# Rounded down products in six of sixteen groups of a sort stage

## The reference

```python
x = x + 0.5 * _L0_ffn_ref(_layernorm(x), expert_sel, keys, values)    # first time
x = x + _L0_attn_ref(...)                                              # linear attention
x = x + 0.5 * _L0_ffn_ref(_layernorm(x), expert_sel, keys, values)    # second time: the first sort stage
x = x + 0.5 * _L1_ffn_ref(...)                                         # mixture of 8 experts, top 2
x = x + _L1_attn_ref(...)
x = x + 0.5 * _L1_ffn_ref(...)
```

```python
gates = sigmoid(xt @ expert_sel.T)                   # all but the top 4 set to 0: gate_full
scores = relu(einsum('nd,edf->nef', xt, keys)) * gate_full[:, :, None]
out = einsum('nef,efv->nv', scores, values)
```

## Time and profile before

| | us |
|---|---|
| median of 3 runs | 1647.75 (1647.23 to 1655.29) |
| profiled execution, its own time | 1646.87 |
| span of its core | 1645.1 |
| first to last gating of the first sort stage (L1520) | 400.8 to 627.6 |
| TensorE, VectorE, ScalarE, GpSimd busy | 1442.1, 1345.3, 1026.5, 856.8 |

### The profile page before, as it was taken

The page is one execution under the profiler, slowest core; times in us unless marked ns, Lnnn a source line. Parts: engine busy times, 40 slices in busy tenths (PEclk is TensorE's granted clock), DMA queues, the critical chain, the costliest instruction groups (busy, mean ns, idle before and its releaser), DMA issues.

```text
span 1645.1 us, 28122 instructions
## 1 busy us (share of the span) xinstructions
PE 1442.1 (88%) x8269; PEld 1095.3 (67%) x8269; DVE 1345.3 (82%) x3897; ACT 1026.5 (62%) x2300; POOL 856.8 (52%) x745
## 2 busy tenths in 40 slices
PE   5999998997999995999639999999999899779991
PEld 4777877654666663999527666666666666459880
DVE  7599998666667776888779999999999867768887
ACT  7544442365323233889668999999999723259880
POOL 5856662210133334467646666666666215537772
PEclk9999998999999997999869999999999999879995
DMA  9992001000011103222199900000000001122225
GB/s 196 179 177 34 1 6 48 1 1 1 26 33 33 45 19 89 60 74 74 49 212 181 163 1 1 2 1 1 1 1 2 1 14 36 43 56 74 72 59 153
DMA packets 156499, 91.24 MB, mean 55 GB/s; under 512 B 19414, under 2 KB 151207, under 8 KB 156353
## 3 DMA queue, kind: packets, MB, share of 16 engines
q1 hardware_dynamic: 142464, 70.52, 22.3%
q0 software_dynamic: 9664, 16.89, 3.2%
q10 hardware_dynamic: 4224, 2.10, 0.4%
HBM read 31.93 MB, written 60.53 MB: 56 GB/s over the span
## 4 chain that ended last, share of the span: by engine, by line
PE 55%; issue 12%; DVE 12%; POOL 10%; ACT 8%; DMA 2%; POOLq 0%; SPq 0%; DVEq 0%; ACTq 0%
PE psum L1379 9%; POOL answers L2443 8%; PE psum L2829 8%; PE psum L2854 5%; PE psum L661 5%; PE psum L662 4%; PE psum L663 4%; ACT psum L2935 4%; DVE psum L2955 3%; PE psum L2807 2%; PE psum L2808 2%; PE psum L2809 2%; PE psum L1134 1%; PE psum L1136 1%; PE psum L1135 1%
## 5 line engine op out<-in xcount | busy, mean ns | idle before, releaser
L2935 ACT ACTIVATE psum<-psum,gate 128x128 f32<-128x128 f32 (+7 forms) x512 | 368.6, 729 | 33.2 <-DVE gate L2955 31.5
L2955 DVE CUSTOM_DVE_ANT_0 psum<-psum,cmask 128x128 f32<-128x128 f32 (+7 forms) x512 | 371.0, 791 | 12.7 <-PE psum L2829 11.4
L1379 PE MATMUL psum<-raw_all,w 128*128 128x512 f32 x384 | 195.4, 592 | 1.5 <-DVE raw_all L1522 1.5
L661 PE MATMUL psum<-xl,wreg 128*128 128x512 f32 x320 | 181.6, 567 | 2.8 <-ACT psum L2935 1.5
L1520 DVE SCALAR_TENSOR_TENSOR raw_all<-psum,hg 128x512 f32<-128x512 f32 x128 | 88.1, 690 | 57.3 <-PE psum L663 55.2
L662 PE MATMUL psum<-xh,wreg 128*128 128x512 f32 x320 | 126.9, 397 | 0.0
L663 PE MATMUL psum<-xh,wreg 128*128 128x512 f32 x320 | 126.7, 396 | 0.0
L2829 PE MATMUL psum<-hh,hl 64*128 64x384 f32 (+3 forms) x768 | 114.4, 373 | 12.7 <-ACT psum L2935 12.7
L2829 PE MATMUL psum<-spare_sets_room 64*128 64x384 f32 (+3 forms) x768 | 114.0, 369 | 12.3 <-ACT psum L2935 12.3
L2443 POOL DMA_INDIRECT answers<-ed,xl x90 | 99.9, 1109 | 31.1 <-issue 30.8
L2829 PEld LDWEIGHTS psum<-hh,hl 64*128 64x128 f32 x768 | 86.3, 190 | 40.7 <-ACT psum L2935 33.7
(11 more groups left out here) (440 smaller groups left out, 4220.9 us busy)
## 6 DMA issues: line engine op xcount, KB each, us to landing
rows<-blank SPq DMA_DIRECT2D x146, 258.0 KB, 6.7
xl<-rows SPq DMA_DIRECT2D x58, 193.5 KB
raw_all<-answers SPq DMA_DIRECT2D x32, 256.0 KB, 4.1
w<-in_L_ffn_W_dram SPq DMA_DIRECT2D x16, 256.0 KB
x<-in_L_attn_x_dram SPq DMA_DIRECT2D x4, 512.0 KB, 5.6
out_dram<-x ACTq DMA_DIRECT2D x8, 256.0 KB, 4.1
answers<-ed,xl POOLq DMA_INDIRECT x90
answers<-row,xl POOLq DMA_INDIRECT x84
```

What stands on the lines that cost most here:

```text
L661: pe.matmul(dst, wh, xl[:, blk(i)], start=start, stop=False)
L1379: pe.matmul(bank(B_OUT[i % 2]), col(dn, j), hidden[:, n % HID, :], start=(j == 0), stop=(j == nf - 1)).then_inc(S["dn_done"], 1)
L2935: return act.activation(src, src, ACT.Exp, bias=kept_at(arg, u, q, a), scale=-1.0, accum_out=kept_at(esum, u, q, a))
L2955: return dve.tensor_tensor_reduce(src, src, mask, 1.0, 3e38, ALU.add, ALU.min, kept_at(arg, u, q, a))
```

## The change

In the first sort stage, the down products of groups 0, 1, 11, 13, 14 and 15 of each block (`THRICE`) become three rounded matmuls. ScalarE casts the gated values of such a group to their high half (`high`, at the head of its period (i, j)), VectorE subtracts for the low half (`low`, behind the gating of the next group). The halves lie in two rooms that take turns (`parted`); a cast or a subtraction waits until the down product of the group that had the room before is done (`wait_parted`). The rooms are in `parts_room` for block 0, in the places of experts 7 and 6 in `m_up` for blocks 1 and 2, in `spare_sets_room` from block 3 on. The unrounded weights are loaded only for groups 2 to 10 and 12 (`ONCE`), by eight DMAs instead of four. `staged` has one place instead of two: the load of an expert waits for the split of the one before. The experts are staged in another order (5 first).

```diff
+    feat_mem = ExitStack()
+    feat_odd = sb("feat_odd", [P, BT, NCH, P + 1 + HPC], F32, feat_mem)
+    feat_mem.close()
+    parts_room = sb("parts_room", [P, BT * NCH * (P + 1 + HPC)], F32R, scope)
...
+    THRICE = (0, 1, 11, 13, 14, 15)
+    ONCE = [(2, 11), (12, 13)]
...
-    staged = w32[:, 3, :].rearrange("p (a w n) -> p a w n", a=2, w=2)
+    MOE_ORDER = (5, 0, 1, 2, 3, 4, 6, 7)
+    staged = w32[:, 3, 2 * P:2 * P + 2 * F1].rearrange("p (w n) -> p w n", w=2)
...
-            wait_past(sp, M["split"], e - 1)
+            wait_past(sp, M["split"], e)
+            k = MOE_ORDER[e]
...
+        def parted(i, j):
+            a = nth(i, j) % 2
+            if i >= NB // 2 - 1:
+                return [spare_sets_room[:, (2 * a + k) * BLK:(2 * a + k + 1) * BLK] for k in range(2)]
+            if i == 0:
+                return [parts_room[:, (2 * a + k) * BLK:(2 * a + k + 1) * BLK] for k in range(2)]
+            return [m_up[:, k, blk(E1 - 1 - a)] for k in range(2)]
+
+        def wait_parted(e, i, j):
+            if nth(i, j) >= 2:
+                k, m = divmod(nth(i, j) - 2, len(THRICE))
+                e.wait_ge(S["dn_done"], k * nf + THRICE[m] + 1)
...
+                if thrice(j):
+                    high, low = parted(i, j)
+                    pe.wait_ge(S["hid_lo"], nth(i, j) + 1)
+                    pe.matmul(bank(B_OUT[i % 2]), col(f_dnl, j), high, start=(j == 0), stop=False)
+                    pe.matmul(bank(B_OUT[i % 2]), col(f_dnh, j), low, start=False, stop=False)
+                    pe.matmul(bank(B_OUT[i % 2]), col(f_dnh, j), high, start=False, stop=(j == nf - 1)
+                              ).then_inc(S["dn_done"], 1)
+                    return
...
+            def high(i, j):
+                act.wait_ge(S["hid_done"], i * nf + j + 1)
+                wait_parted(act, i, j)
+                act.activation(parted(i, j)[0], hidden[:, (i * nf + j) % HID, :], ACT.Copy).then_inc(S["hid_hi"], 1)
...
+                    if i < NB and thrice(j):
+                        high(i, j)
                     if i == 0 and closing:
                         closing.scalar(act, j)
...
+            def low(i, j):
+                dve.wait_ge(S["hid_hi"], nth(i, j) + 1)
+                wait_parted(dve, i, j)
+                high, rest = parted(i, j)
+                dve.tensor_tensor(rest, hidden[:, (i * nf + j) % HID, :], high.bitcast(F32), ALU.subtract
+                                  ).then_inc(S["hid_lo"], 1)
...
                     if i < NB:
                         apply_gates(i, j)
+                    n = i * nf + j - 1
+                    if 0 <= n < NB * nf and thrice(n % nf):
+                        low(*divmod(n, nf))
                     if i == 0 and closing:
                         closing.vector(dve, j)
...
-                sp.dma_start(f_dn.rearrange("p (j d) -> p j d", j=NF0)[k * E0:(k + 1) * E0], values[k]
-                             ).then_inc(S["w_load"], 16)
+                for lo, hi in ONCE:
+                    sp.dma_start(f_dn.rearrange("p (j d) -> p j d", j=NF0)[k * E0:(k + 1) * E0, lo:hi], values[k][:, lo:hi]
+                                 ).then_inc(S["w_load"], 16)
```

More of the change, by code:

```diff
@@ L329, in build @@
     setup_mem.close()
-    feat_odd = sb("feat_odd", [P, BT, NCH, P + 1 + HPC], F32, scope)
+    feat_mem = ExitStack()
+    feat_odd = sb("feat_odd", [P, BT, NCH, P + 1 + HPC], F32, feat_mem)
+    feat_mem.close()
+    parts_room = sb("parts_room", [P, BT * NCH * (P + 1 + HPC)], F32R, scope)
     kvbd = sb("kvbd", [P, BATCH, 2, P], F32, scope)
@@ L988, in build @@
     MOE_AT = 7
-    staged = w32[:, 3, :].rearrange("p (a w n) -> p a w n", a=2, w=2)
+    MOE_ORDER = (5, 0, 1, 2, 3, 4, 6, 7)
+    staged = w32[:, 3, 2 * P:2 * P + 2 * F1].rearrange("p (w n) -> p w n", w=2)
     def moe_sems():
-        return {"load": [sem(f"moe_load{a}") for a in range(2)], "cast": sem("moe_cast"), "split": sem("moe_split")}
+        return {"load": sem("moe_load"), "cast": sem("moe_cast"), "split": sem("moe_split")}
     def moe_load(sp, M):
@@ L997, in moe_load @@
         for e in range(E1):
-            wait_past(sp, M["split"], e - 1)
-            sp.dma_start(staged[:, e % 2, 0], W1[:, e, :]).then_inc(M["load"][e % 2], 16)
-            sp.dma_start(staged[:, e % 2, 1].rearrange("p (q d) -> p q d", q=BT), W2[:, blk(e, BT), :]).then_inc(M["load"][e % 2], 16)
+            wait_past(sp, M["split"], e)
+            k = MOE_ORDER[e]
+            sp.dma_start(staged[:, 0], W1[:, k, :]).then_inc(M["load"], 16)
+            sp.dma_start(staged[:, 1].rearrange("p (q d) -> p q d", q=BT), W2[:, blk(k, BT), :]).then_inc(M["load"], 16)
     def moe_high(act, M, e):
-        act.wait_ge(M["load"][e % 2], 32 * (e // 2 + 1))
-        act.activation(m_up[:, 0, blk(e)], staged[:, e % 2, 0], ACT.Copy)
-        act.activation(m_dn[:, 0, blk(e)], staged[:, e % 2, 1], ACT.Copy).then_inc(M["cast"], 1)
+        act.wait_ge(M["load"], 32 * (e + 1))
+        k = MOE_ORDER[e]
+        act.activation(m_up[:, 0, blk(k)], staged[:, 0], ACT.Copy)
+        act.activation(m_dn[:, 0, blk(k)], staged[:, 1], ACT.Copy).then_inc(M["cast"], 1)
     def moe_low(pool, M, e):
         pool.wait_ge(M["cast"], e + 1)
-        pool.tensor_tensor(m_up[:, 1, blk(e)], staged[:, e % 2, 0], m_up[:, 0, blk(e)].bitcast(F32), ALU.subtract)
-        pool.tensor_tensor(m_dn[:, 1, blk(e)], staged[:, e % 2, 1], m_dn[:, 0, blk(e)].bitcast(F32), ALU.subtract
+        k = MOE_ORDER[e]
+        pool.tensor_tensor(m_up[:, 1, blk(k)], staged[:, 0], m_up[:, 0, blk(k)].bitcast(F32), ALU.subtract)
+        pool.tensor_tensor(m_dn[:, 1, blk(k)], staged[:, 1], m_dn[:, 0, blk(k)].bitcast(F32), ALU.subtract
                            ).then_inc(M["split"], 1)
@@ L1271, in sort_sems @@
         if first:
-            names += ("routed", "gate_in", "cleared", "max_done", "top_set", "rest_set", "gate_set")
+            names += ("routed", "gate_in", "cleared", "max_done", "top_set", "rest_set", "gate_set", "hid_hi", "hid_lo")
         S = {n: sem(f"{ph}_{n}") for n in names}
@@ L1344, in col, with thrice, nth @@
             return w[:, j * P:(j + 1) * P]
+        def thrice(j):
+            return first and j in THRICE
+        def nth(i, j):
+            return i * len(THRICE) + THRICE.index(j)
+        def parted(i, j):
[9 more added lines that the diff above has]
+                e.wait_ge(S["dn_done"], k * nf + THRICE[m] + 1)
         def tensor(pe):
@@ L1377, in down_product @@
                 if first and n == 0:
-                    pe.wait_ge(weights, 16 * (P // E0))
+                    pe.wait_ge(weights, 16 * len(ONCE) * (P // E0))
+                if thrice(j):
[6 more added lines that the diff above has]
+                    return
                 pe.matmul(bank(B_OUT[i % 2]), col(dn, j), hidden[:, n % HID, :], start=(j == 0), stop=(j == nf - 1)
@@ L1749, in sync @@
             for k in range(P // E0):
-                sp.dma_start(f_dn.rearrange("p (j d) -> p j d", j=NF0)[k * E0:(k + 1) * E0], values[k]
-                             ).then_inc(S["w_load"], 16)
-            sp.wait_ge(S["w_load"], 16 * (P // E0))
+                for lo, hi in ONCE:
+                    sp.dma_start(f_dn.rearrange("p (j d) -> p j d", j=NF0)[k * E0:(k + 1) * E0, lo:hi], values[k][:, lo:hi]
+                                 ).then_inc(S["w_load"], 16)
+            sp.wait_ge(S["w_load"], 16 * len(ONCE) * (P // E0))
         def gpsimd(pool):
```

## The result

| | before | after |
|---|---|---|
| median of 9 runs each, us | 1647.75 (1645.01 to 1655.29) | 1654.19 (1650.67 to 1658.72) |
| ratio of the times | | 1.0041, 95% interval 1.0021 to 1.0060 |
| profiled execution, its span | 1646.87, 1645.1 | 1650.83, 1649.1 |

The forecast was 1647.8, with 1641.5 to 1654.0 around it. The kernel became slower by 0.4%, where no change was forecast; the median lies 0.2 us above the range.

A forecast was written before the change was run, and what follows sets the result against it. The stage was taken as bound by TensorE. Terms 1.0 + 0.5 + 0.75 - 2.0 - 0.2 = +0.05 us on the profiled 1646.87, with the median 0.9 above, gave 1647.8; range for 8 in 10: 1641.5 to 1654.0.

The forecast's parts named there:

- Down 11 is due at 3.34. No wait: Block boundary, us after group 11's up product mark: subtraction 11 ends at 3.29, before its down product is due.
- the walk: Step-by-step timing of a block boundary, from group 11's up product to group 4's in the next block: 14.59 us.
- The boundary, "gives 0.29": Each block boundary gets 0.29 us shorter, not 1.18, as two waits take the rest; seven boundaries: -2.0.
- The two waits: At each boundary, down 14 and down 15 wait for late subtractions, 0.28 and 0.60 us; the latter behind the gate copy.
- Product 11 of block 7, -0.2: In the last block, rounding the down product of group 11 saves 0.2 us.
- Opening, +1.0: Start of block 0: subtractions ahead of the query stage's quotient delay the projection by 1.23; down 1 returns 0.2: +1.0 us.
- Block 0, end, +0.5: End of block 0: an extra query-stage subtraction behind subtraction 11 delays the expert choice and the spreading of gates: +0.5 us.
- Block 2, +0.75: Block 2: POOL's split of expert weights lengthens VectorE's subtraction 11; cost between 0 and 1.05 us, taken as +0.75 once.
- Weights staged singly, hidden: Weight staging in the first sort stage: later expert loads and eight DMAs instead of four stay hidden, costing nothing.
- loop: Rival, chance 0.10: casts waiting for the two rooms form a serial loop at the boundaries, 12 us slower: 1659.8.
- The row sends: Rival, chance 0.06: subtractions lengthen POOL's row sends by 1.05 us each, two at the end, +2.1: 1649.9.
- The saving does arrive: Rival, chance 0.12: the lows are never late and 45 down products save 0.197 us each, 8.9 less: 1638.9.

The follow-up runs named there:

- low_last: Changed kernel with the matmul that needs VectorE's low half put last of the three and waited for alone; stage 225.46 us, ratio to the kernel before 0.9997.
- copy_first: Changed kernel with ScalarE's copy of the next block's gates put ahead of the cast of group 15; stage 227.83 us, ratio to the kernel before 1.0009.

## Why the prediction was wrong, by its own steps

- **"Down 11 is due at 3.34. No wait"**: this is the step that failed. It took a down product to need its halves when its first matmul starts, 0.23 after U. The wait stands ahead of that product's weight load, and in the row at 575.81 the load starts at U. Due is then 3.11, and the subtraction of the walk ends at 3.29. In the trace it ends 0.16 after U13; that costs 0.08 before the first matmul and 0.08 between the first and the second: 1.53 for 1.37. In the other blocks the period is 1.52 to 1.56, and 1.68 and 1.64 in blocks 2 and 7. low_last, where the first two matmuls need the cast alone, brings it back to 1.36 to 1.39 in every block. By the Trainium skill (TensorE: Matmul & The Clock Gate, "Architectural detail: the array is 16× 32×32, not 1× 128×128") TensorE can pull a weight load ahead of matmuls in flight; the load at 575.81, which starts together with the up product's third matmul, agrees.
- **The boundary, "gives 0.29"**: it cost 0.12 (blocks 3 to 6 are 28.39 long in the mean, 28.27 before). From U11 to the next U4 the walk gave 14.59, before took 14.88, and after 15.02 from block 3 to block 4. Of the 0.43 missed, 0.17 is product 11; 0.07 is the restart at down 14, and 0.14 the turning back (1.93 from U2 to U3 where 1.79 was walked), which waits for a copy queued behind the cast of group 1. The two waits and their causes were right: low_last took the first away, copy_first the gate copy, and both together brought 0.97 a block. Seven boundaries: +0.9 instead of -2.0, which is 2.9 of the 3.6 us missed.
- **Product 11 of block 7, -0.2**: the same error, and more of it. Block 7 from U0 to U15 is 0.48 longer; 0.34 of that is the boundary's share behind U0 (7.00 for U0 to U4, where before has 6.66), which leaves +0.14. In this block VectorE is behind with its gatings (the subtraction starts at 622.69), and the halves come 0.27 after U13 instead of 0.16.
- **Opening, +1.0**: U0 to U4 went from 7.79 to 8.85, +1.06. The first down product starts 1.42 later than before, counted from U0, and the projection 1.21 (forecast: 1.4 and 1.23); the wait of 1.18 in the earlier trace rows is there again, at 407.91. The 0.6 that another order of VectorE's list takes back confirm it.
- **Block 0, end, +0.5**: block 0 is 1.37 longer, less 1.06, plus the 0.22 that a boundary gives back before U0: 0.53. No experiment took this one away.
- **Block 2, +0.75**: 29.39 - 28.41 = 0.98, within the bounds 0 and 1.05. That the split falls on this chain was right, the victim was not: the subtraction took 0.82 (forecast 1.4), and the larger part came from the one-column operation behind it, which was not in the sum. The forecast took the split's place in the block as fixed; in the changed kernel's third profile it lay 0.36 us later, the subtraction took 1.19, and the block lost 1.37, above the upper bound.
- **Weights staged singly, hidden**: right (0.9998, every block the same).
- **The range.** The sum by measured terms is 1.06 + 0.53 + 0.98 + 0.84 + 0.14 = 3.55, of 3.63 measured. That would be 1651.3 and in the range: a wrong mechanism, and still a number inside. The rest up to 1654.19 is no term of the sum. The forecast put the median 0.9 above the profiled execution, as it was before, but after it lies 3.4 above it; whether that is scatter of the runs or a loss outside the stage is open. The comparison of a kernel with itself (1.0009, up to 1.0028) shows that some us belong in such a range for the runs alone.
- **Rivals.** No loop: the room's wait is there in each boundary (1.11 before the cast at 575.61), but it is not passed on from one to the next. The row sends hardly became longer: 967 ns in the mean after, 965 before, though one in block 2 took 1122. The saving does arrive once the order is changed, 0.97 of 1.18 a block.

## What to carry to other kernels

A product's operands are due when its weight load would be issued, one matmul earlier than its own start; a walk has to set deadlines there. What a missed one costs was here the whole time from that deadline to the end of the late operand (0.16, 0.35 and 0.59), with no separate term for a restart. When a product is split over engines, give the latest half to the last of its matmuls, and put a copy that other engines wait for ahead of a cast that itself waits: the same work, in another order, went on one chip from 1.0044 to 0.9971, with the opening and the split moved as well. Where terms of tenths are multiplied by the number of blocks, one deadline decides the sign: where one is met by under 0.1 (here by 0.05), carry both outcomes into the range, multiplied as well.

## What the runs showed of the hardware

- A wait on a semaphore ahead of a matmul holds its weight load too (574.55, released by the subtraction that ended at 574.43, in place of 573.85). After it the first and the second matmul are 0.30 to 0.32 apart instead of 0.23 or 0.24, even where, as at 567.41, the release came before the matmul's own due time. A load only 0.05 after U (down 13: U at 570.76, first matmul at 570.99) left no such mark.
- VectorE's and GpSimd's operations with two operands in SBUF met with unequal cost: 0.82 for 0.68, 1.73 for 1.27 and 1.10 for 0.15. What VectorE's operation paid went by how much of GpSimd's was left when it started, and not by its own size: the subtraction ended 0.55 after the half that it met, whether it started 0.27 or 0.64 before that half's end, and the one-column operation ended 0.02 after the second half, of which 1.08 was left.
- The start of the stage scatters between 394.7 and 400.4 us over the profiled executions, and its length, in the kernel before and its unedited copy, by 0.07 (226.79 and 226.72). In the changed kernel's three profiles it is 230.42, 230.34 and 230.78, with the 0.4 in block 2. The lengths of single blocks told edits of 0.5 us apart, where the whole time did not.
